# Turning and adding gathered rows and edge attributes in PSUM instead of adding them on VectorE

## What is computed

```
x_j = x[src] + edge_attr                    # 80,000 x 128
k = (x_j @ wk.T + bk).reshape(-1, 4, 32)
q = (x[dst] @ wq.T + bq).reshape(-1, 4, 32)
alpha = sum(q * k, axis=-1) / sqrt(32)      # 80,000 x 4
```

## Time and profile before

| | us |
|---|---|
| median of three runs | 12611.91 |
| lowest and highest of these | 12582.9, 12612.57 |
| span of the profiled execution, first to last instruction | 12521.9 |
| the three score passes in it, together | 3485 |

### The profile page before, as it was taken

How to read it: one execution, slowest core, us unless ns; L and a number is a source line. 1 busy time by engine, 2 the same in 40 slices (tenths; PEclk the granted TensorE clock), 3 DMA queues, 4 the chain that set the end, 5 groups by cost and what they waited for, 6 DMA issues and landing times. The chain is left out here.

```text
span 12521.9 us, 164892 instructions
## 1 busy us (share of the span) xinstructions
PE 6604.1 (53%) x35059; PEld 5552.8 (44%) x35060; DVE 5536.9 (44%) x13969; ACT 2372.4 (19%) x5039; POOL 6320.5 (50%) x6362
## 2 busy tenths in 40 slices
PE   4555686555686555785335333433533353355555
PEld 3555674555665555663223222333322332234444
DVE  4444664444664444753334233433433343345555
ACT  1222452222452222452000000000000000011111
POOL 2555432556422555423663666366366636635663
PEclk7777898777897777896556555655655565567777
DMA  2333321334322333321111111111111111112221
GB/s 81 113 113 113 99 80 55 116 114 118 101 69 64 114 115 114 102 63 29 44 44 55 46 42 43 56 44 43 47 53 44 43 57 43 43 25 87 82 80 58
DMA packets 697724, 893.26 MB, mean 71 GB/s; under 512 B 148412, under 2 KB 442581, under 8 KB 697500
## 3 DMA queue, kind: packets, MB, share of 16 engines
q0 software_dynamic: 198368, 429.61, 13.4%
q1 hardware_dynamic: 497412, 461.38, 11.8%
q10 hardware_dynamic: 1848, 1.12, 0.0%
HBM read 698.40 MB, written 193.14 MB: 71 GB/s over the span
## 5 line engine op out<-in xcount | busy, mean ns | idle before, releaser
L761 POOL DMA_INDIRECT l_sums_ring<-table_typed,index x2512 | 2436.2, 970 | 1951.2 <-ACT index L862 1181.2
L897 PE MATMUL psum<-l_sums_ring,select 128*128 x6720 | 1630.0, 419 | 3214.3 <-DVE select L793 2600.8
L761 POOL DMA_INDIRECT acc<-table_x,index x2016 | 2039.8, 1012 | 2141.2 <-DVE index L756 1556.4
L897 PEld LDWEIGHTS psum<-l_sums_ring,select 128*128 128x128 f32 x6720 | 1404.0, 309 | 3443.1 <-issue 3443.1
L823 DVE TENSOR_TENSOR acc<-acc,psum 128x128 f32 (+1 forms) x4032 | 1160.8, 288 | 3336.4 <-remote 2288.8
L793 DVE TENSOR_TENSOR select<-iota_row,dst_local 128x512 f32<-128x512 f32 (+1 forms) x1680 | 1070.8, 638 | 340.0 <-issue 318.8
L1015 PE MATMUL psum<-ident,select 128*128 128x128 f32 x2016 | 437.8, 356 | 1465.0 <-DVE acc L974 593.5
L990 DVE TENSOR_TENSOR l_scores_prod<-l_scores_key,psum 128x512 f32<-128x512 f32 x504 | 345.7, 686 | 1777.3 <-ACT l_scores_key L963 1303.7
L862 ACT COPY index<-tile_idx 128x4 int32 (+1 forms) x785 | 150.3, 193 | 4510.2 <-remote 2770.2
L1015 PEld LDWEIGHTS psum<-ident,select 128*128 128x128 f32 x2016 | 300.3, 181 | 1540.3 <-issue 827.3
L761 POOL DMA_INDIRECT l_pass_ring<-table_kv,index x672 | 674.7, 1004 | 598.5 <-issue 242.4
(11 more groups left out here) (319 smaller groups left out, 10103.9 us busy)
## 6 DMA issues: line engine op xcount, KB each, us to landing
acc<-in_edge_attr_dram SPq DMA_DIRECT2D x2016, 64.0 KB
rows_dram<-l_scores_mixT SPq DMA_DIRECT2D x504, 256.0 KB
l_values_ring<-rows_dram SPq DMA_DIRECT2D x504, 256.0 KB
table_typed<-l_rows_rows SPq DMA_DIRECT2D x40, 1024.0 KB, 4.2
l_sums_ring<-table_typed,index POOLq DMA_INDIRECT x2512
acc<-table_x,index POOLq DMA_INDIRECT x2016
l_pass_ring<-table_kv,index POOLq DMA_INDIRECT x672
table_x<-l_rows_rows SPq DMA_DIRECT2D x40, 256.0 KB, 2.2
```

The costliest lines, as they stand in the source:

```text
L761: pool.indirect_dma_start(out=ring[:, at, u, :], out_offset=None, in_=table, in_offset=bass.IndirectOffsetOnAxis(ap=index[:, at % REGIONS, ...
L897: ins = pe.matmul(sums(r, u), select[:, r, u, :], rows, start=True, stop=True)
```

## The change

VectorE's addition of `attr` to `ring` goes, with its semaphore. PE turns both by products with the identity and accumulates the two in one PSUM bank: for each of the four blocks a product of `ring` that starts the sum and a product of `attr` that ends it. The waits for the gather and for the attributes move from DVE to PE, between the transposes of `select` and these products. SP's next load of attributes waits for the turn of the region that last used the buffer, where it waited for its addition.

```diff
                         def load(i, r):
-                            at_least(sp, p_mixed, region_of(i, r) - (REGIONS - 1))
+                            at_least(sp, p_turned, region_of(i, r) - (REGIONS - 1))
...
                             make_select(dve, i, r)
-                            dve.wait_ge(gathered[r], landed(i, base[r]))
-                            dve.wait_ge(p_in[r], (i + 1) * (16 * GROUP))
-                            dve.tensor_tensor(ring[:, r, :, :], ring[:, r, :, :], attr[:, r, :, :], ALU.add).then_inc(p_mixed, 1)
...
                             j = region_of(i, r)
-                            pe.wait_ge(p_mixed, j + 1)
+                            pe.wait_ge(p_selected, j + 1)
                             at_least(pe, p_spread, j)
                             for u in range(GROUP):
                                 pe.transpose(psum[:, 0, u * P:(u + 1) * P], select[:, r, u, :], ident[:])
+                            pe.wait_ge(gathered[r], landed(i, base[r]))
+                            pe.wait_ge(p_in[r], (i + 1) * (16 * GROUP))
                             for u in range(GROUP):
-                                ins = pe.transpose(psum[:, 1, u * P:(u + 1) * P], ring[:, r, u, :], ident[:])
+                                at = slice(u * P, (u + 1) * P)
+                                pe.matmul(psum[:, 1, at], ring[:, r, u, :], ident[:], start=True, stop=False)
+                                ins = pe.matmul(psum[:, 1, at], attr[:, r, u, :], ident[:], start=False, stop=True)
                             ins.then_inc(p_turned, 1)
```

More of the change, by code:

```diff
@@ L919, in queries @@
                     return psum[:, 4 + 2 * (r % 2):6 + 2 * (r % 2), 0:pair * Q_W].rearrange("p a (b w) -> p a b w", w=Q_W)
-                with block(name, p_index, p_selected, p_mixed, p_turned, p_spread, p_projected, p_evacuated, p_multiplied, p_scored,
+                with block(name, p_index, p_selected, p_turned, p_spread, p_projected, p_evacuated, p_multiplied, p_scored,
                            p_score_kept, *p_in, *p_out) as b:
```

## The result

The changed kernel takes **12866.7 us** (median; 12857.2 to 12880.6), the kernel before 12612.2 (12582.9 to 12630.2), with four runs each: a ratio of **1.0206, 95% interval 1.0194 to 1.0218**, or +254 us. Its profiled execution has a span of 12857.0 us.

What follows compares the result with a forecast made beforehand. The score passes were taken as bound by POOL's serial gathers plus waits for indices behind held PE completions; +244 - 65 = +179 us on the 12521.9 span, plus a 90 us constant, gave 12790, range 12480 to 13110.

Steps and rivals of the forecast that it cites:

- Runs of two regions, each with a hold: Score passes: POOL's gather runs shrink from three regions to two, 14.8 us per run, +0.49 us a region, +244 us; chance 0.60.
- The count of matmuls as what decides: Score passes: PE completions are held by matmuls since the run began; 24 pass, 32 are held, the change makes 36.
- DVE loses the addition: worth nothing by itself: Score passes: removing 0.68 us a region from DVE gains nothing there, as DVE is busy 3 us of 6.9.
- POOL's relief, -65 us: Score passes: gathers no longer lengthened by the addition; half of 131 us assigned to it, bounds 0 and 131.
- The constant of 90 us: Whole program: median of runs lies 90 us above the profiled span, carried unchanged from 12701 to 12791.
- The moved waits cost nothing: Score passes: waits for gather and attributes moved to PE, and SP's load wait, bounded by 0 and 40 us, taken as 0.
- Runs of three: Rival, score passes: hold goes by time or a higher limit, three-region runs stay, only POOL's relief is left, 12547; chance 0.26.
- the 4.1 that I gave for the full clock: Score passes: at full clock a run's first products would end 4.1 us after its start and, by time, pass.
- PE did not become the bound: Rival, score passes: at half clock PE's 36 matmuls take 7.7 us a region and set the pace, +333 us, 12945; chance 0.10.
- Runs of one region: Rival, score passes: even a run's first turn is held, 9.8 us a region, +1457 - 65 us, 14000; chance 0.04.

Runs made afterwards that it cites:

- the wide products: Kernel before, addition and waits kept, plus two unread fp32 products of 512 columns (four matmuls) in PE's turn each region; ratio 1.0106.
- six products alone: Kernel before, addition and waits kept, plus six unread fp32 products of 128 columns (12 matmuls) in PE's turn each region; ratio 1.0092.
- without attributes: Changed kernel with its waits and no addition, but PE only transposes the gathered rows as before, leaving attributes out of the sum; ratio 1.0119.
- the control: Kernel before with one more register operation ahead of two waits of the sum passes, score passes untouched; ratio 0.9999.
- the long pause: Kernel before with an unread 128x512 subtraction on POOL after each region's four gathers in the score passes; ratio 0.9722; with the change too, 0.9765.

## Why the prediction was right, and where it was not

The time (12790 forecast, 12867 measured), the direction and the pattern were right; part of the reason was not, and that the time came so near is in part luck, as shown below.

*Runs of two regions, each with a hold.* Right. Forecast were 14.8 us for two regions (10.0 for eight gathers, 1.0 for the hold, 3.8 to the next run). At the median, a run took 9.71 us and the wait after it 5.18, together 14.9. The first products reached ACT 1.8 us after the run's end, near the far end of my 0 to 2.0, but the way from there to the next run took 3.4 us in the timeline shown (1013.66 to 1017.02), not 3.8.

*The count of matmuls as what decides.* **This step failed.** Four matmuls in the wide products did what twelve did, and with 24 matmuls as before all first products were held once the addition was gone. What the runs showed in its place are two conditions: PE's work since the start of a run, and whether POOL was slowed or stood in it. The change worsens both. Its two halves cost +0.9% (six products alone) and +1.2% (the addition gone and the waits moved, without attributes), and the change +2.1%. That the two are weighed against each other by one rule is my reading and not shown.

*DVE loses the addition: worth nothing by itself.* On DVE it was worth nothing, as forecast. Beside POOL it had a use: with a reduction in its place, and all else kept, runs of twelve fell from 114 in the control to 31. I had seen the effect and booked it as a pure hindrance. In time that kernel lost nothing, so how much of the 1.2% is the addition's, and how much VectorE's and SP's waits', stays open.

*POOL's relief, -65 us.* The gathers gave back 114 us, near the 131 that I named as the bound; by the gathers that start under each, the addition's share in the trace of before was 87 us and the comparison's 45, not half and half. But it did not belong in the sum: the 10.0 us of a run of eight were already made of the median gather of the earlier trace rows, so the -65 us were counted twice. Without them, and with 3449 / 504 = 6.84 us a region for before (my windows in the earlier trace rows were 36 us too wide in all), the sum is (7.4 - 6.84) x 504 = +282 us against the 300 us measured in the passes (275 beside the control's).

*The constant of 90 us.* Not work around the span. In the changed kernel the span is 1.8 us below the time of its execution (12857.0 and 12858.8); the profiled execution of before was itself a short one. The median after is 10 us above its span, so +254 us on the medians stand beside +335 on the spans, 36 of them in the transformer pass. That is how a sum that was too small by 120 us on the passes came within 77 us of the time: two errors that offset each other.

*The moved waits cost nothing.* Borne out for PE's waits where the addition stays (1.0000). Without it they can't be told from its absence, and SP's and VectorE's were never moved alone.

*The rivals.* Runs of three did not stay, and the clock did rise, from 0.75 to 0.86 in the passes, without letting the first products pass: the held ones end some 4.3 us after the start of their run, near the 4.1 that I gave for the full clock, and 233 of 249 are held. So the hold does not go by time alone. The rule that I cited from the Trainium skill's "TensorE: Matmul & The Clock Gate", section "Part 4: PE-mode transpose", would have the clock rise with products in place of transposes; that it rose does not bear the rule out, since with six products more and all transposes kept it is 0.84 in the first pass. PE did not become the bound: it is idle for some 30% of the passes. Runs of one region were 23 of 262.

**What stays open** is what holds a completion of PE while POOL gathers. The trace calls it "remote" and names nothing. Its record of semaphore updates puts the delay ahead of ACT: for the held completions of the changed kernel the increment is recorded 7.2 us after the products' end, and ACT starts 0.02 us behind it (medians). The ends of matmuls are modelled, so whether the products or their signal are late is not shown. That a pause of POOL of 1.27 us ends the holds was shown (none of 504, with the change and without); one of 0.74 us shortens them and the waits, by how much differs between two chips (waits of 1543 us without a pause, 1090 and 893 with it). Whether it is POOL's issuing or the transfers that it starts, which a pause spaces out too, was not separated.

## What to carry to other kernels

Where POOL gathers without a gap and another engine's completions are "remote" and late, look at what makes POOL stop before counting work on the other engines: an operation that seems to be in its way may let such a completion through. Before taking work off an engine that is not the bound, ask what that work does to its neighbours. A pause costs a few lines and is worth a try: 0.64 ms of useless work on POOL made this kernel 2.8% faster.

## What the runs showed of the hardware that was not expected

- Completions of PE's products are held while POOL issues indirect DMAs back to back (in the changed kernel for 7.3 us at the median of those held, in the trace of before for up to 12.1 us), and for at most 2.1 us when POOL does 1.27 us of other work after every four of them.
- A subtraction of 128x512 on POOL, SBUF to SBUF, takes 1274 ns in the score passes (the long pause) and 1040 in the value passes of the same trace. The two read their second input in different patterns, so it is not shown that the pass makes the difference.
- A gather that starts under an operation of DVE with two inputs in SBUF takes 1134 to 1266 ns on average, one that starts under a reduction or under a product with one input in PSUM 946 (trace of before).
- The granted clock in the score passes went from 0.75 to 0.86 with the change, and to 0.95 with the change and the long pause (the window of the first pass of that kernel; the 0.95 is the clock):

```profile
189.00:1250.00 1061.00, 785.05 (x5991) 723.37 (x5992) 400.31 (x827) 275.38 (x499) 877.15 (x840) 0.95 0.42 124
```
